# Two-layer relational graph convolution on one core: where x is loaded, and at which steps three sets of work are placed

## The reference, cut to what matters

```python
def _rgcn_conv(x, src, dst, etype, W, root, b):
    seg = dst * num_rel + etype
    sums = segment_sum(x[src], seg); cnt = segment_sum(ones, seg)
    mean = (sums / maximum(cnt, 1.0)[:, None]).reshape(num_nodes, num_rel, -1)
    return einsum('nri,rio->no', mean, W) + x @ root + b

h = relu(_rgcn_conv(x, src, dst, edge_type, W1, root1, b1))
x = _layernorm(x + _rgcn_conv(h, src, dst, edge_type, W2, root2, b2))
```

## Time and profile before

| | |
|---|---|
| median of three runs | 1575.47 us |
| the profiled execution's own time | 1582.24 us |
| its span | 1580.4 us |
| mean granted TensorE clock, of full speed | 0.976 |
| TensorE busy | 94% |
| VectorE, ScalarE, GpSimd busy | 65%, 36%, 40% |
| TensorE's products (line 720) in the chain that ended last | 45% |

### The profile page before, as it was taken

One profiled execution on the slowest core, in us unless ns is written; L12 is line 12 of the kernel. 1 busy time (PEld: TensorE's weight loads), 2 busy tenths in 40 slices (PEclk: granted clock), 3 DMA queues, 4 the chain that ended last, 5 costly groups with the idle time before them and its releaser, 6 DMA issues.

```text
span 1580.4 us, 23799 instructions
## 1 busy us (share of the span) xinstructions
PE 1485.0 (94%) x9014; PEld 1462.6 (93%) x9014; DVE 1022.3 (65%) x1599; ACT 572.7 (36%) x818; POOL 629.2 (40%) x455
## 2 busy tenths in 40 slices
PE   6999998999999998999989799999999999899995
PEld 5999998999999998998989799999999999899995
DVE  6899999955777765885971022545454545478797
ACT  3222111112444543584552111333333334258542
POOL 1121112223677774664620310434343424366561
PEclk9999999999999998999999899999999999999998
DMA  4353221243677766765423441656565555576443
GB/s 163 114 189 123 83 74 34 71 140 112 190 245 218 215 206 210 221 201 160 142 85 130 150 149 42 197 157 203 167 197 172 190 182 184 171 234 202 137 138 124
DMA packets 102645, 249.79 MB, mean 158 GB/s; under 512 B 12607, under 2 KB 75758, under 8 KB 102486
## 3 DMA queue, kind: packets, MB, share of 16 engines
q0 software_dynamic: 31680, 131.81, 27.5%
q1 hardware_dynamic: 70870, 116.69, 22.2%
HBM read 204.47 MB, written 65.49 MB: 171 GB/s over the span
## 4 chain that ended last, share of the span: by engine, by line
PE 58%; DVE 20%; DMA 12%; POOL 4%; issue 3%; ACT 2%; SPq 0%; DVEq 0%; ACTq 0%; POOLq 0%
PE prod L720 45%; PE agg L747 11%; DMA y<-y_stage 5%; DMA raw<-y,bucket_index 5%; DVE slot_hot L1214 3%; POOL raw L474 2%; DVE ranks L1169 2%; DVE ranks L1164 2%; DVE keyed L1222 2%; POOL scale L482 1%; DVE dst_hot L1215 1%; DVE g_low L989 1%; PE prod L711 1%; DMA x_rows<-in_x 1%; DVE g_low L986 1%
## 5 line engine op out<-in xcount | busy, mean ns | idle before, releaser
L720 PE MATMUL prod<-w_high,h_high 128*128 128x384 f32 x2160 | 736.3, 341 | 20.2 <-ACT y_stage L622 12.8
L720 PE MATMUL prod<-w_low,h_high 128*128 128x384 f32 x2160 | 730.4, 338 | 0.0
L720 PE MATMUL prod<-w_high,h_low 128*128 128x384 f32 x2160 | 729.7, 338 | 0.0
L474 POOL DMA_INDIRECT raw<-y,bucket_index x380 | 492.8, 1297 | 559.5 <-DVE g_low L989 296.8
L989 DVE TENSOR_TENSOR g_low<-raw,g_high 128x768 fp32r<-128x768 f32 x280 | 259.1, 954 | 306.6 <-ACT g_high L589 305.8
L720 PEld LDWEIGHTS prod<-w_high,h_high 128*128 128x128 f32 x2160 | 412.3, 191 | 22.8 <-ACT y_stage L622 15.4
L720 PEld LDWEIGHTS prod<-w_low,h_high 128*128 128x128 f32 x2160 | 411.8, 191 | 0.0
L720 PEld LDWEIGHTS prod<-w_high,h_low 128*128 128x128 f32 x2160 | 411.5, 191 | 0.0
L622 ACT ACTIVATE y_stage<-prod 128x384 f32<-128x384 f32 x280 | 137.5, 492 | 702.4 <-PE prod L720 639.7
L589 ACT ACTIVATE g_high<-raw 128x768 fp32r<-128x768 f32 x300 | 243.2, 842 | 106.8 <-DMA raw<-y,bucket_index 87.6
L747 PE MATMUL agg<-g_high,one_hot 128*128 128x384 f32 x760 | 202.5, 348 | 22.6 <-DVE g_low L989 20.6
(11 more groups left out here) (138 smaller groups left out, 772.1 us busy)
## 6 DMA issues: line engine op xcount, KB each, us to landing
y<-y_stage SPq DMA_DIRECT2D x280, 187.5 KB
w_raw<-in_w_all SPq DMA_DIRECT2D x36, 1152.0 KB
raw<-y,bucket_index POOLq DMA_INDIRECT x380, 5.3
x_rows<-in_x SPq DMA_DIRECT2D x10, 375.0 KB
y<-in_x SPq DMA_DIRECT2D x1, 3750.0 KB, 14.8
y<-acc SPq DMA_DIRECT2D x10, 375.0 KB
acc<-in_x SPq DMA_DIRECT2D x10, 375.0 KB
out<-acc SPq DMA_DIRECT2D x10, 375.0 KB
```

What stands on the lines that cost most here:

```text
L474: pool.indirect_dma_start(raw[:, i % NRAW, :], None, y[0:written * N, :], bass.IndirectOffsetOnAxis(ap=bucket_index[:, at_column:at_column ...
L720: mm = pe.matmul(prod[:, bank, 0:HALF], left[:, k, t * P:(t + 1) * P], right[:, h, k, :], start=(k == 0 and left is h_high and right is w_ ...
```

## The change

x is loaded into `acc` by GpSimd's queue, two tiles ahead of the bias addition, once all turns of h are made and h is stored; SP's queue no longer has these loads. The turns of h come two steps behind their product instead of one, so the last two fall into steps 0 and 1 of matrix 9. The sums of the sixth group are placed at steps 4, 4, 5, 5, 6, 6, 7, 7, 8 and 9 of matrices 7 and 16 (before: 1, 2, 3, 4, 5, 6, 6, 7, 8 and 9). Those of the eighth group are placed at steps 5, 6, 7, 9, 10, 12, 13, 15, 16 and 18 of matrix 8, and at steps 4, 5, 6, 7, 8, 10, 11, 12, 13 and 15 of matrix 17. GpSimd's wait for h's stores moves from ahead of the seventh group's gathers to ahead of the loads of x.

```diff
+    AHEAD = 2
         def averaging(g, r, n):
             def actions(s):
-                todo = [("sum", g, r, t) for t in range(T) if s == (t + 1 if t < 6 else t)]
+                todo = [("sum", g, r, t) for t in range(T) if s == 4 + 5 * t // (T - 1)]
...
         def last_sums(g):
-            return lambda s: [("sum", g, R - 1, t) for t in range(T) if s == 3 + (STEPS - 5) * t // (T - 1)]
+            first, steps = (5, 13) if g < R else (4, 11)
+            return lambda s: [("sum", g, R - 1, t) for t in range(T) if s == first + steps * t // (T - 1)]
...
         def completing(s):
-            turn = [("turn", 1, None, T - 1)] if s == 0 else [("turn", 2, None, s - T - 1)] if s > T else []
+            turn = [("turn", 1, None, T - 1)] if s == 0 else [("turn", 2, None, s - T - 2)] if s > T + 1 else []
...
-        def last_turn(s):
-            return [("turn", 2, None, T - 1)] if s == 0 else []
+        def last_turns(s):
+            return [("turn", 2, None, T - 2 + s)] if s < 2 else []
...
             for s in range(STEPS):
                 store_y(R - 1, 1, s)
-                if s == 3:
-                    sp.wait_ge(transposed, 6 * T)
-                    sp.wait_ge(h_stored, 16 * T)
-                if 3 <= s < 3 + T:
-                    t = s - 3
-                    sp.dma_start(acc[0:ROWS[t], t, :], x[t * NT:t * NT + ROWS[t], :])\
-                        .then_inc(residual_loaded[t], 16)
...
+            def load_residual(t):
+                pool.dma_start(acc[0:ROWS[t], t, :], x[t * NT:t * NT + ROWS[t], :]).then_inc(residual_loaded[t], 16)
+
             pool.wait_ge(bias_loaded, 32)
+            pool.wait_ge(transposed, 6 * T)
+            pool.wait_ge(h_stored, 16 * T)
+            for t in range(AHEAD):
+                load_residual(t)
             for t in range(T):
+                if t + AHEAD < T:
+                    load_residual(t + AHEAD)
                 pool.wait_ge(residual_loaded[t], 16)
                 pool.tensor_tensor(acc[:, t, :], acc[:, t, :], bias[:], ALU.add).then_inc(x_biased, 1)
...
-            pool.wait_ge(h_stored, 16 * T)
             gather_relation(2 * R - 2, 0)
```

More of the change, by code:

```diff
@@ L690, in _ @@
             matrix(MEAN1, None, None, completing, spilled=(0, R - 1), ahead=True, high_at=0)
-            matrix(ROOT2 - 1, R - 1, banks(2), last_turn)
+            matrix(ROOT2 - 1, R - 1, banks(2), last_turns)
             matrix(ROOT2, None, None)
@@ L917, in _ @@
             matrix(ROOT2 - 1, banks(2), lambda s: kept(2 * STEPS, (root_kept, 2 * STEPS), 2)(s) if s < BANKS
-                   else staged(R - 1)(s) + ([(h_low_ready, 2 * T * 2 + 2 * s + 2)] if s < T else []), last_turn)
+                   else staged(R - 1)(s) + ([(h_low_ready, 2 * T * 2 + 2 * s + 2)] if s < T else []), last_turns)
             matrix(ROOT2, banks(2), lambda s: [(y_staged, STEPS * R - BANKS + s + 1) if s < BANKS
@@ L1318, in _ @@
             matrix(MEAN1, completing, keep_mean1, spilled=(0, R - 1), low_at=((1, 0, K), (13, 0, K // 2), (16, K // 2, K)))
-            matrix(ROOT2 - 1, last_turn)
+            matrix(ROOT2 - 1, last_turns)
             for s in range(STEPS):
```

## The result

Five runs of the kernel after have a median of 1563.26 us (1554.7 to 1568.14), five of the kernel before on the same chip 1577.26 us (1573.15 to 1580.7). The ratio is 0.990, 95% interval 0.9863 to 0.9937: faster by 14 us, where 25 were forecast and the range ended at 1561. The profiled execution has a span of 1566.4 us, again 14.0 under that of before.

What follows compares the result with a forecast made beforehand. TensorE was taken as the bound almost everywhere, so only its waits could go. Terms of -14, -7, -6 and +2 us summed to -25, from 1575.5 to a median of 1550.5 us, range 1541 to 1561.

Steps and rivals of the forecast that it cites:

- part A: Matrices 7 and 16: later sums of the sixth group cover the gathers' late start; -7 us, bounds 0 and -14.
- part C: Matrix 9 and matrix 10's start: x by GpSimd's queue ends the waits behind SP's queue; -14 us.
- part B: Matrix 8: later first sums and turns two steps behind remove waits; -6 us, bounds -2 and -9.
- part D: Matrix 17 and the end: unbroken rows of sums make the output's end later; +2 us, bounds -2 and +6.
- four double steps: Matrices 7 and 16: four steps carrying two sums each cost 4.9 us over the floor in all.
- At worst 880 beside the loads of x: Matrix 9: weights need 9.2 us and land near 876, at worst 880, so step 16 does not wait.
- Relu gets a second step of distance, so these go: Matrix 8: waits of first sums and at turns go, among them 1.48 us for relu and 3.14 for VectorE.
- R1: Rival for matrices 7 and 16: double steps gain nothing, each 2.6 us over the floor; 1557.5 us, chance 0.16.
- Covers the gathers' late start: Matrices 7 and 16: first low part comes 12.3 us in, step 4's product ends 15.6 us in at the earliest.
- R2: Rival for matrix 9: transfers, not their place in SP's queue, hold the steps; 1562.5 us, chance 0.08.
- R3: Rival for the end: gathers do not keep pace with five sums in a row, +8 us; 1556.5 us, chance 0.10.
- R4: Rival: GpSimd's own loads of x make it slower; 1585 us at 10.5 us a tile, chance 0.02.

Runs made afterwards that it cites:

- x_late: Kernel after, with GpSimd's loads of x held until the first weight half of matrix 10 has landed; median 1563.49 us, ratio 0.9908 against the kernel before.
- C alone: Kernel before with only x loaded by GpSimd's queue, two tiles ahead; median 1568.23 us, ratio 0.9924 against the kernel before.
- relu_first: Kernel after, with ScalarE's relu ahead of the staging of the same step; median 1558.46 us, ratio 0.9868 against the kernel before.
- the table of four: Four kernels: matrix 8's sums at old or new steps, turns one or two steps behind; matrices 8 and 9 together take 179.0, 179.7, 173.3 and 176.5 us.
- sixth_mid: Kernel after, with the sixth group's sums at steps 3, 4, 4, 5, 6, 6, 7, 8, 8, 9; median 1566.85 us, ratio 0.9885 against the kernel before.
- out_pool: Kernel after, with the ten output stores issued by GpSimd's queue; ratio 0.9911 against the kernel before.

## Why the prediction was wrong

The forecast of a gain held, its size did not: 14 us instead of 25. Each of the four terms had the right sign, and each fell short of its gain or went over its cost: 4.9 us of the gap are part A's, 3.3 part C's, 2.5 part B's and 0.9 part D's; 0.6 us gained elsewhere go against them. The steps that failed are the price of four double steps in A, the price of the late turns and the row taken for the weights in C, and the slow product and the second wait that B left out.

- **Part C (-14, measured -10.7 in the whole change, -12.5 alone).** The reading of SP's queue was right: one queue of stores and loads at 4.5 us a pair set the steps, and without the loads the steps behind step 8 take TensorE's 3.12 us up to step 14. Two things were left out. "At worst 880 beside the loads of x" took a row without such loads for the weights; they took 16.1 us instead of 9.2, and were issued some 3 us later behind step 8's start than forecast, because the y stores were held as well (shown by `x_late`: 8.1 us, and an issue 4.3 us behind it). That is the 1.5 us that C alone lacks. And the late turns were costed "about 1.3 us" and hidden by a wait at step 8. Steps 0 to 2 take 15.5 us where they took 11.7, 3.8 more: 0.7 is the turn itself, 1.31 a second wait for relu (the other of 1.31 was there before) and 1.40 VectorE's; 0.4 is left over. The wait at step 8 took in only 1.9 of it: steps 0 to 7 took 31.1 us instead of 29.2, and passed the point at which the queue would have held them: 858.2 against 818.05 + 38.3 = 856.35.
- **"Relu gets a second step of distance, so these go"** held in matrix 8, where no staging stands in ScalarE's order, and brought no time there. **"The wait of 1.31 us in matrix 9 goes too"** failed: relu for a turn in a step of matrix 9 stood behind that same step's staging, whichever tile it was, so two late turns had two such waits (shown by `relu_first`).
- **Part B (-6, measured -3.5, of which 0.7 is the turn that went to matrix 9).** What it gains comes from the places of the sums (the table of four), about 1.4 us in the first ten steps and 2.1 in the others. What it had too low: the first pair of sums costs 3.0 us behind it (796.47), not 2, and the product behind it runs partly at 1.2 GHz (granted clock 0.81 over 797 to 806), which makes step 15 7.8 us long, 1.6 over the floor. The sum had nothing for that, though the kernel before has the same (step 16, 7.8 us, 0.79 over 809 to 817) and the bound of -2 names it. The second pair cost 1.77 us, as forecast. The second wait marked "issue", 2.23 us (738.78), was in no term.
- **Part A (-7, measured -2, and -1.2 by the means)** failed most; R1 (0) is nearest. The one double step of the kernel before is a poor model for four in a row: it came almost 30 us behind the first gather (616.58, 645.40). "Covers the gathers' late start" overlooked that gathers stop after five raw buffers until the first sum is prepared. So waits moved from steps 1 and 2 into steps 5, 6 and 10. The four double steps were to cost 4.9 us over the floor of 5.96 each; they cost 5.8 in matrix 7 and 7.0 in matrix 16, and step 10, at 6.7 and 6.2 us (before 4.9), 1.8 and 1.3 more. That the stand-still of GpSimd makes them long is shown in matrix 16 alone (`sixth_mid`).
- **Part D (+2, measured +2.9 in the pair and +2.6 over all profiles)** was right. What sets it stays open; the queue that stores the output accounts for 1.6 us at most.
- **R2** has its mechanism, at an eighth of its price. The rule on the Trainium skill's page "DMA: Bandwidth & Descriptors", section "Issuing engines are not separate DMA queues", would have had C near 0: the runs measured -12.5 alone. That the engines are shared shows in one stretch, from 859 us on, where a y store takes 4.6 us instead of 1.5, and the weights, with the engines 98% busy, twice as long.
- **R3 and R4** did not come: the end moved by 3 us, and a tile of x landed 5.7 to 7.8 us behind its issue, with up to three in flight.

The range of 1541 to 1561 ends 2 us below the median. Its width took the misses of A, B and C as if they came one at a time; they came together, in one direction.

## What to carry to other kernels

A queue whose issues are paced by its own transfers is a serial resource even when the 16 DMA engines are mostly free (0.33 busy here); move what isn't urgent to another queue, but look at what else is in flight when a large urgent load goes out. When a consumer is moved later to cover a slow start, check that the producer can run ahead that far: with five buffers it stops, and here the wait came back a few steps later. To give an action distance, move it in the order of the engine that performs it, not only in the step number of the one that uses it.

## What the runs showed of the hardware

- SP's queue alone, with tiles of 125 rows, kept the share of the 16 DMA engines at 0.33 and moved 128 to 131 GB/s in three kernels (before, after, `x_late`). While weights of 128 rows came from the same queue in `x_late`, slices of 0.22 us show up to 419 GB/s. The kernel after, 842 to 856 us:

```profile
842.00:856.00 14.00, 14.00 (x83) 14.00 (x82) 1.20 (x1) 1.13 (x3) 1.06 (x2) 1.00 0.33 130
```

  The Trainium skill's page "DMA: Bandwidth & Descriptors", section "Why a DMA increments its semaphore by 16 and not by 1", says that a transfer is split over the largest number of engines up to 16 that divides its rows. For 125 rows that would be 5 of 16, an estimated share of 0.31; the trace's 0.33 agrees. Whether tiles of 128 rows would free SP's queue was not tried.
- GpSimd's plain loads and stores cost it 0.5 to 0.6 us of issue each, less than the 1.0 to 1.5 that was estimated from a gather. The last store of the output in `out_pool`:

```profile
1550.80 0.53 POOL L569 DMA_DIRECT2D out<-acc  x1 [0.18 <-issue]
```
